# Where the first context is loaded, and six more filler matmuls in the opening of a fused attention and feed-forward kernel

## The reference, cut to what matters

```python
def _layernorm(x, axis=-1, eps=1e-05):
    m = jnp.mean(x, axis=axis, keepdims=True)
    v = jnp.var(x, axis=axis, keepdims=True)
    return (x - m) / jnp.sqrt(v + eps)

# x: (8, 256, 256) f32, ctx_1024: (8, 120, 256) f32
def xattn(x, w1, v1, w2):                 # all three are ctx_1024
    x1 = jnp.einsum('eth,efh->etf', x, w1)
    x2 = jnp.einsum('eth,efh->etf', x, v1)
    h = jax.nn.gelu(x1, approximate=True) * x2
    return jnp.einsum('etf,efh->eth', h, w2)

def ffn(x, ...):                          # 256 -> 1024 -> 1024 -> 1024 -> 256
    h = silu(x @ w1.T * w1_s) * (x @ w2.T * w2_s)
    h = gelu(h @ h1.T * h1_s)
    h = gelu(h @ h2.T * h2_s)
    return h @ w3.T * w3_s

x = x + xattn(_layernorm(x), ctx_1024, ctx_1024, ctx_1024)
x = x + ffn(_layernorm(x), ...)
```

## Time and profile before

| | us |
|---|---|
| median of 3 runs | 333.95 |
| lowest and highest | 333.41, 333.95 |
| the profiled execution, its own time | 334.1 |
| its span (first to last instruction) | 332.3 |
| TensorE busy with matmuls | 324.5 (98% of the span) |
| VectorE, ScalarE, GpSimd busy | 264.6, 218.1, 47.3 |

### The profile page before, as it was taken

The page is one execution under the profiler, slowest core; times in us unless marked ns, Lnnn a source line. Parts: engine busy times, 40 slices in busy tenths (PEclk is TensorE's granted clock), DMA queues, the critical chain, the costliest instruction groups (busy, mean ns, idle before and its releaser), DMA issues.

```text
span 332.3 us, 4771 instructions
## 1 busy us (share of the span) xinstructions
PE 324.5 (98%) x1643; PEld 274.4 (83%) x1643; DVE 264.6 (80%) x492; ACT 218.1 (66%) x367; POOL 47.3 (14%) x86
## 2 busy tenths in 40 slices
PE   7999999999999999999999999999999999999994
PEld 4699888888878888888998888888887888888994
DVE  3577888796996999998579666398899798987594
ACT  2355838648596886778914564977679687785840
POOL 6247020201100022112130003000100000110000
PEclk9999999999999999999999999999999999999999
DMA  7769999949657762735306033345575863443003
GB/s 227 257 208 292 207 225 368 407 172 306 192 176 250 284 240 90 228 129 155 100 0 231 24 126 126 128 127 189 189 225 197 278 249 130 126 131 123 0 32 104
DMA packets 23213, 60.22 MB, mean 181 GB/s; under 512 B 1680, under 2 KB 7184, under 8 KB 20880
## 3 DMA queue, kind: packets, MB, share of 16 engines
q0 software_dynamic: 13728, 37.75, 38.0%
q1 hardware_dynamic: 9168, 21.60, 19.0%
q10 hardware_dynamic: 288, 0.51, 0.5%
HBM read 49.36 MB, written 6.29 MB: 167 GB/s over the span
## 4 chain that ended last, share of the span: by engine, by line
PE 95%; DVE 1%; DMA 1%; POOL 1%; issue 0%; ACT 0%; DVEq 0%
PE P L1290 61%; PE P L1242 18%; PE P L1319 9%; PE P L1214 2%; PE P L1198 2%; PE P L1206 2%; DMA xs<-in_x 1%; POOL rs L434 1%; PE P L1391 1%; PE P L1384 1%; PE P L1398 0%; PE P L1329 0%; DVE xn L819 0%; POOL rs L432 0%; DVE xs L831 0%
## 5 line engine op out<-in xcount | busy, mean ns | idle before, releaser
L1290 PE MATMUL P<-TR,WR 128*128 128x512 f32 x896 | 205.5, 390 | 0.0
L1290 PEld LDWEIGHTS P<-TR,WR 128*128 128x128 f32 x896 | 167.7, 188 | 35.4 <-DVE H L915 0.8
L591 ACT ACTIVATE TR<-H 128x512 fp32r<-128x512 f32 x112 | 68.1, 626 | 29.1 <-DVE H L894 26.4
L899 DVE TENSOR_TENSOR TR<-H,TR 128x512 fp32r<-128x512 f32 x112 | 73.8, 686 | 7.6 <-ACT TR L591 5.9
L1242 PE MATMUL P<-X,W 128*128 128x512 f32 (+1 forms) x320 | 62.7, 351 | 0.1
L1242 PEld LDWEIGHTS P<-X,W 128*128 128x128 f32 x320 | 51.7, 189 | 8.1 <-DVE X L836 0.5
L894 DVE TENSOR_TENSOR H<-H 128x512 f32<-128x512 f32 x64 | 42.0, 684 | 0.0
L872 DVE SCALAR_TENSOR_TENSOR H<-P,sc,SLY 128x512 f32<-128x512 f32 (+1 forms) x40 | 25.2, 639 | 19.1 <-ACT SLY L581 10.0
L581 ACT ACTIVATE SLY<-P,sc 128x512 f32<-128x512 f32 (+1 forms) x40 | 23.7, 601 | 18.6 <-PE P L1242 18.4
L605 ACT ACTIVATE H<-P 128x512 f32<-128x512 f32 x48 | 27.8, 593 | 11.6 <-PE P L1290 11.6
L625 ACT ACTIVATE H<-H,sc 128x512 f32<-128x512 f32 x40 | 27.4, 713 | 10.7 <-DVE H L915 10.7
(11 more groups left out here) (72 smaller groups left out, 197.9 us busy)
## 6 DMA issues: line engine op xcount, KB each, us to landing
WR<-blocks_h POOLq DMA_DIRECT2D x16, 1024.0 KB, 5.1
WR<-in_h POOLq DMA_DIRECT2D x12, 1024.0 KB, 5.2
H<-in_h POOLq DMA_DIRECT2D x8, 512.0 KB, 12.0
blocks_h<-H SPq DMA_DIRECT2D x4, 1024.0 KB, 6.6
SLY<-in_h SPq DMA_DIRECT2D x8, 512.0 KB, 4.5
SLY<-in_w SPq DMA_DIRECT2D x6, 512.0 KB, 4.6
W<-in_w POOLq DMA_DIRECT2D x4, 512.0 KB, 7.8
WR<-in_w POOLq DMA_DIRECT2D x2, 1024.0 KB, 5.1
```

What stands on the lines that cost most here:

```text
L591: eng.activation(TR[:, f % RING, 0, :], operand(c, L, s, kk), ACT.Copy).then_inc(s_hi, 1)
L899: eng.tensor_tensor(TR[:, f % RING, 1, :], operand(c, L, s, kk), TR[:, f % RING, 0, :].bitcast(f32), ALU.subtract).then_inc(s_lo, 1)
L1290: out_ = eng.matmul(bank(c, L, s, m)[:, :], WR[r % WRING][:, at:at + 128], TR[:, f % RING, h, :], start=(s in FRESH[L] and kk == 0 and h = ...
```

## The change

The first context's two loads leave ScalarE's queue. SyncE issues them now, by its own functions `load_cf` and `load_ct`, behind batch 1 and ahead of the scales; for t = 0 these functions wait for nothing. Five of the six spins grow, by 1, 1, 1, 2 and 1: six matmuls more, 43 in place of 37.

```diff
-SPIN = (16, 2, 2, 1, 14, 2)
+SPIN = (16, 3, 3, 2, 16, 3)
...
             for j in range(2):
                 eng.dma_start(xs[:, j, :], x_v[0, :, j, :]).then_inc(s_x0[j], 16)
             load_x(1)
+            load_cf(0)
+            load_ct(0)
             eng.dma_start(sc[:, :], cols).then_inc(s_sc, 16)
...
             table(ACT.Gelu_apprx_tanh)
-            eng.dma_start(cf[:, 0, :, :, :], ctx_feat[:, 0, :, :, :]).then_inc(s_cf[0], 16)
-            eng.dma_start(ct[:, 0, :, :], ctx_tok[:, 0:2, :]).then_inc(s_ct[0], 16)
             copy_half(0)
```

## The result

The change makes the kernel slower. Median 336.09 us (5 runs, 334.99 to 336.87) against 333.41 us for the kernel before (5 runs, 332.43 to 333.95); the ratio of the runs is 1.0089, 95% interval 1.0064 to 1.0114. Forecast were 333.9 us and no measurable difference, with a range from 332.4 to 334.6. What happened is the outcome of rival 3, the late context, to which the prediction gave 0.10, though not by its working.

A forecast was written before the change was run, and what follows sets the result against it. TensorE was taken to bound the kernel, with a fixed tail from layer1. Load gain -0.43, spins +0.13 and +0.21, the rest 0: -0.09 us, from 333.95 to 333.9 us; range 332.4 to 334.6.

The forecast's parts named there:

- rival 3: Opening: cf waits behind batch 1, lands near 8.0 us, score_half(0) starts 0.8 to 1.1 us late; 334.9 us; chance 0.10.
- Is the context now late?: Opening, SyncE's queue: cf lands at 6.6 us, ct near 7.4, both in time for TensorE; cost zero, cover thin.
- so W12 lands as before: Opening, W12's load: the DMA engines carry the same bytes by 12 us, so its landing does not move.
- Rival 1: Opening: a smaller gap before turn_half(0,0) raises TensorE's clock sooner; 1.1 us gained, 332.9 us; chance 0.34.
- The load's gain: Batch 0's halves land sooner without the context beside them; 0.43 us gained, bounded at 0.45 by GpSimd's W12 issues.
- The spins: Six added spins in the opening: 0.21 us each cold, 0.11 warm; 0.13 and 0.21 us reach the path, the rest zero.
- The fixed tail: From layer1 (15.87 us) on, TensorE's matmuls keep their length, 316.4 us; the end moves one to one with layer1's start.
- The baseline: Starting time for the forecast: median 333.95 us, with the profiled execution at 334.1 us, 0.15 us above it.

The follow-up runs named there:

- W12 later: Changed kernel with GpSimd issuing the four W12 pieces behind the first normalisation's two rstd halves instead of ahead: 332.69 us, ratio 0.9983 against the kernel before.
- the wait filled: Changed kernel with ten more spins between turn_half(0,1) and score_half(0), where TensorE waited for cf: 334.92 us, ratio 1.0046 against the kernel before.
- the move alone: Changed kernel with the spins of before (16, 2, 2, 1, 14, 2), context on SyncE's queue: 335.87 us, ratio 1.007 against the kernel before.
- The 26 spins: Kernel before with 26 spins instead of 16 ahead of turn_half(0,0): 333.69 us, ratio 1.0006.
- the spins alone: Kernel before with the change's six more spins, context still on ScalarE's queue: 332.98 us, ratio 1.0001.
- W12 later with the context on ScalarE's queue: Kernel before, spins of before, with GpSimd's W12 loads issued behind the two rstd halves: 333.71 us, ratio 1.0002.
- The two kernels with more spins at the start: Kernel before with 19 or 26 spins instead of 16 ahead of turn_half(0,0): 333.20 us (ratio 0.9998) and 333.69 us (1.0006).
- one early piece of W12: Changed kernel with one W12 piece (512 KB) ahead of the rstd halves and three behind: 335.31 us, ratio 1.0054 against the kernel before, without the 662.39 us run.

## Why the prediction was wrong

**The step that failed** is "Is the context now late?". It put cf's landing at 6.6 us, from the row of the same load in a burst from one queue, and took 6.9 as the other bound; it landed at 8.8, and ct at 10.8 instead of 7.4. In the burst at 12.4 to 14.2 us SyncE's queue had the DMA engines to itself. At 4 us it doesn't: W12, 2 MB in GpSimd's queue, starts at 3.7 us, before cf is under way, and between 5 and 8 us W12 moves 0.53 MB to q1's 0.31 MB. In packets the two are near even (143 and 171), but W12's are of some 3.7 KB each and q1's of 1.8 KB. The prediction said that the DMA engines carry the same bytes by 12 us, "so W12 lands as before", and left it there. True of the bytes, but who comes first within these 12 us was the whole question, and before the change it was the context; and W12 didn't stay where it was either, its packets came 1.1 us sooner. On its own queue the context took turns with batch 0 at once and was nearly through when W12 began. The experiment with W12 later shows this: same order, same queue, cf at 5.4.

**Rival 3** named the right outcome and was sized too small: 8.0 for cf against 8.8 measured, and 334.9 - 333.95 = 1.0 us for the whole kernel against 2.7. That its 8.0 comes near is in part luck. It let cf wait for batch 1 until 6.44, but batch 1 landed at 1.64 + 3.2 = 4.8; and it gave q1 150 KB per us beside W12, where between 5 and 8 us it moved about 100. Its "against" (the same 512 KB ahead, no q10 to serve) left W12 out. It also had only the wait in it. The wait has a second price that no rival named: the clock falls, 1.0 us by the profile of the kernel with the wait filled.

**Rival 1** was half right. The upper level did come earlier, by 7.3 us, with the first gap at 0.42 us. That the smaller gap brought it is not shown: in the move alone the level rose at 4.6 us, ahead of any gap. What the early rise gave, the later wait took back. The Trainium skill ("TensorE: Matmul & The Clock Gate", section "HAM oscillation — how this bites in real kernels") describes a like case: waits for a DMA between bursts of matmuls throttle the engine again. The profile after goes the same way, with 1.00, then 0.50, then 1.00, though its wait of 1.54 us is shorter than those of the page's example.

**The load's gain** was right: 0.43 us forecast at GpSimd's rs, 4.49 - 4.02 = 0.47 measured, with the bound at GpSimd's W12 issues where it was put. Once those are moved too, rs comes at 3.69.

**The spins** were right in their price, 0.21 us each when cold, and nothing measured speaks against their weight: no difference in the time of the kernel, twice (1.0001 against the kernel before; 332.69 and 332.70 with W12 later). The second of these has a cover that the prediction didn't have, the wait for W12 in `layer1`. And 0.34 us is less than the intervals can tell from nothing; in the changed kernel SPIN[2] ran at the upper level besides.

**The fixed tail** was not quite fixed. Of the 2.7 us, 0.55 us were lost between 86 and 102 us, where ScalarE waited 0.5 us longer for the load of the weights' test. The 26 spins show that this needs no late opening; why the load lands sooner in one run than in another stays open.

**The baseline** was off too. The three times shown lay in the upper part of what the kernel before does (332.1 to 335.8 over all sessions). The forecast was made against 333.95, while the medians since are 332.9 to 333.7. The profiled execution that it was read from has a late rise of the clock (10.6 us), and so have those of the spins alone (10.2) and of W12 later with the context on ScalarE's queue (10.4), which took 334.85 and 334.78 us and lie 1.9 and 1.1 us above the medians of their kernels. So the profile of before may show the slower half of what that kernel does.

Open as well: how much the clock's moment has to do with that spread. The two kernels with more spins at the start had an early rise in their profile and no better median. And W12 behind the context in SyncE's own queue, which would order all the loads by need, stays untested. Two kernels for it, with the new spins and with the old, gave no time: W12 is float32 in memory and float32r on the chip, and only GpSimd may issue a load that converts.

## What to carry to other kernels

A transfer's time to land depends on what runs beside it as much as on its size and its place in its own queue (cf took 3.3 and 6.7 us from the same place): before taking a duration from elsewhere in a trace, look at which other queues had packets under way there and which will have them here. When a load is moved, ask what starts at the moment at which it used to be finished; here moving the bulk load behind it repaired the change, while reordering the small loads among themselves only chose which of them was late. And price a new wait on TensorE twice, once for its length and once for the clock behind it; here ten filler matmuls in the wait bought the second back.

## What the runs showed of the hardware

One run of the kernel with one early piece of W12 took 662.39 us, twice its usual time. It was the profiled one, and the page shows TensorE at work for all of it, with the engines beside it busy for about as long as ever, in us:

```profile
PE 653.4 (99%) x1649; PEld 451.1 (68%) x1649; DVE 271.5 (41%) x492; ACT 223.0 (34%) x367; POOL 46.4 (7%) x86
```
```profile
20.00:660.00 640.00, 636.12 (x1582) 439.48 (x1580) 264.26 (x469) 218.95 (x358) 38.86 (x64) 1.00 0.28 87
```

The same 1649 matmuls took twice as long (653.4 us against 325.7 in the changed kernel). By their durations TensorE was at about the lower level from the first to the last, under a load that is dense for 640 us; the column of the granted clock says 1.00, as it does for the opening of the kernel before, where the durations say otherwise as well. It happened once in about 200 runs of these kernels, and nothing in the kernel explains it. Where the column and the durations disagree, go by the durations.
